# Sixteen-head windowed attention: mask, maxima and normalisation divided anew among the engines

## The reference

```
q, k = rotary(x @ Wq.T), rotary(x @ Wk.T);  v = x @ Wv.T      # 16 heads of 8
scores = q @ k.T / sqrt(8)
mask = (j > i) | (j < i - (WINDOW - 1))                        # WINDOW = 128
p = softmax(where(mask, -inf, scores))
y = (p @ v) @ Wo.T + bo
```

## Time and profile before

| | |
|---|---|
| median of 3 runs | 1532.76 us (1532.57 to 1542.49) |
| the profiled execution, its own time | 1545.9 us |
| its span, first to last instruction | 1544.1 us |
| PE busy | 1269.2 us, 82% |
| DVE busy | 1046.3 us, 68% |
| ACT busy | 808.2 us, 52% |
| POOL busy | 395.7 us, 26% |
| mean granted TensorE clock | 0.911 of 2.4 GHz |

### The profile page before, as it was taken

How to read it: one execution, slowest core, us unless ns; L and a number is a source line. 1 busy time by engine, 2 the same in 40 slices (tenths; PEclk the granted TensorE clock), 3 DMA queues, 4 the chain that set the end, 5 groups by cost and what they waited for, 6 DMA issues and landing times. The chain is left out here.

```text
span 1544.1 us, 23279 instructions
## 1 busy us (share of the span) xinstructions
PE 1269.2 (82%) x8400; PEld 815.4 (53%) x8400; DVE 1046.3 (68%) x2162; ACT 808.2 (52%) x2180; POOL 395.7 (26%) x248
## 2 busy tenths in 40 slices
PE   5767878887998888789775888889689988988986
PEld 4412335884665556456531233579456654655663
DVE  4789976226887787378449998741378879746853
ACT  2466423453764556466627553336276636665663
POOL 0036633412000332032011665360400023202300
PEclk9789978997999989999987888989799999999997
DMA  8300001780000100001010000068400000000000
GB/s 298 123 0 1 0 1 54 254 268 19 2 1 1 35 21 15 1 15 28 2 28 0 1 0 1 1 201 263 130 1 2 1 1 22 22 1 14 22 8 14
DMA packets 42179, 72.21 MB, mean 47 GB/s; under 512 B 3793, under 2 KB 27473, under 8 KB 41810
## 3 DMA queue, kind: packets, MB, share of 16 engines
q1 hardware_dynamic: 28242, 56.30, 10.8%
q10 hardware_dynamic: 11776, 10.23, 2.6%
q0 software_dynamic: 2048, 4.20, 0.9%
HBM read 51.19 MB, written 13.24 MB: 42 GB/s over the span
## 5 line engine op out<-in xcount | busy, mean ns | idle before, releaser
L912 POOL TENSOR_TENSOR scratch<-scratch 128x1024 f32<-128x1024 f32 x64 | 149.7, 2353 | 140.4 <-DVE scratch L883 119.9
L634 POOL TENSOR_TENSOR small<-small,w_const 128x16 f32<-128x16 f32 x32 | 101.1, 3163 | 298.2 <-DVE small L1753 298.2
L731 PE MATMUL psum<-scratch,w_const 128*128 128x512 f32 x256 | 148.8, 713 | 18.5 <-POOL scratch L912 18.4
L883 DVE TENSOR_TENSOR_SCAN scratch<-psum,scratch 128x512 f32<-128x512 f32 x128 | 150.1, 1206 | 9.5 <-ACT psum L804 8.9
L634 POOL TENSOR_TENSOR rstd<-rstd,w_const 128x4 f32<-128x4 f32 x32 | 32.8, 1029 | 432.9 <-DVE rstd L596 430.3
L1706 ACT ACTIVATE scratch<-psum,mx 128x128 f32<-128x128 f32 x256 | 90.0, 376 | 72.7 <-DVE mx L1794 71.5
L804 ACT ACTIVATE psum<-scratch,a_neg 128x512 f32<-128x512 f32 x128 | 87.8, 690 | 61.2 <-DVE scratch L883 52.1
L1374 ACT ACTIVATE scratch<-psum,mx 128x256 f32<-128x256 f32 (+1 forms) x256 | 111.2, 465 | 10.0 <-DVE mx L1410 8.4
L720 PE MATMUL psum<-scratch,cb 96*128 96x512 bf16 x128 | 49.7, 428 | 60.6 <-DVE scratch L875 51.3
L1160 ACT ACTIVATE scratch<-psum,scratch 128x128 f32<-128x128 f32 x240 | 68.3, 368 | 54.7 <-PE psum L1101 54.6
L1541 PE MATMUL psum<-w_local,hT 128*128 128x512 f32 x192 | 91.2, 615 | 6.3 <-ACT hT L1523 5.1
(11 more groups left out here) (266 smaller groups left out, 3199.6 us busy)
## 6 DMA issues: line engine op xcount, KB each, us to landing
expert_weights<-in_expert_weights SPq DMA_DIRECT2D x61, 512.0 KB, 5.1
scratch<-scratch ACTq DMA_DIRECT2D x48, 128.0 KB, 2.3
folded_products<-expert_weights SPq DMA_DIRECT2D x8, 512.0 KB, 3.1
folded<-folded_products SPq DMA_DIRECT2D x8, 512.0 KB, 4.7
w_local<-in_local SPq DMA_DIRECT2D x1, 3122.0 KB
sorted_y<-scratch ACTq DMA_DIRECT2D x12, 256.0 KB, 5.6
scratch<-sorted_x SPq DMA_DIRECT2D x4, 704.0 KB, 6.7
scratch<-in_cross SPq DMA_DIRECT2D x1, 2624.5 KB, 12.9
```

Source lines behind the costliest of these rows:

```text
L634: t.eng.tensor_tensor(v, v, W("const", "neg_half").to_broadcast([P, v.shape[1]]), ALU.pow).then_inc(t.s[done], 1)
L731: ins = pe.matmul(sum_banks[c], ident, t.m.hC[:, 2 * ((n - 1) % 2) + c, :], start=(n == 1), stop=(n == NS))
L883: dve.tensor_tensor_scan(t.m.hs[:, n % 2, c, :], t.ps["dA"], t.m.dBu[n % 2][:, c, :], 0.0, ALU.mult, ALU.add)\
L912: t.eng.tensor_tensor(t.m.hC[:, 2 * (n % 2):2 * (n % 2) + 2, :], t.m.hs[:, n % 2], C, ALU.mult)\
```

## The change

The mask is no longer written by TensorE. The host constant `band3` is negated once into `hidden` (0 or +1e30), q is negated as it is copied out of PSUM, so the banks hold minus the scores, and the instruction that finds the extremum of a block also adds `hidden` to it, writes the sum back to PSUM and keeps the minimum, which is minus the maximum of the masked scores. That is one `tensor_tensor_reduce` for a block of a half, so four for a wide unit and eight for a narrow one, where there was one reduction. The exponential is taken with scale -1. Maxima, exponentials, inverses and probabilities are signalled by half (u) instead of by unit. The normalisation moves to GpSimd: one multiplication of 128x512 for each half, by the inverse sums spread over the columns. `TURNS` is made anew for all engines.

```diff
 TURNS = {
     "dve": [
...
+        1, 1, 5, 1, 3, 1, 1, 1, 1, 1, 1, 1, 1, 1, 1, 1, 3, 1, 2, 2, 1, 1, 3, 1, 2, 2, 1, 1, 7, 5, 8, 8, 7, 7, 7,
+        7, 7, 7, 7, 7, 7, 7, 7, 7, 7, 7, 7, 7, 7, 7, 7, 7, 13, 3, 8, 6, 3, 1, 5, 1, 1, 1, 1, 6, 3, 1, 1, 2, 1, 2,
...
+        hidden = cbv["band3"]
...
-            dve.tensor_scalar(rank_w[:, :], cbv["band3"][:, P:2 * P], -1.0, 1.0 / P, ALU.is_lt, ALU.mult)
+            yield from t.w.step(dve.tensor_scalar(hidden, hidden, -1.0, None, ALU.mult))
+            dve.tensor_scalar(rank_w[:, :], hidden[:, P:2 * P], 1.0, 1.0 / P, ALU.is_gt, ALU.mult)
...
             def turn(n, u):
                 yield
-                if u == 0:
-                    t.w(t.s["prob_ready"])
+                t.w(t.s["prob_ready"])
...
-                    mask = cbv["band3"][:, (2 - nk) * P:2 * P].rearrange("p (o z) -> p o z", o=1)
-                    for bank in banks:
-                        pe.matmul(bank, cbv["ident"], mask.to_broadcast([P, len(gg), nk * P]), start=True, stop=False,
-                                  skip_group_check=True)
...
-                                            start=False, stop=(a == len(gg) - 1), skip_group_check=True)
+                                            start=True, stop=True, skip_group_check=True)
...
-                    yield
-                    t.w(t.s["max_ready"])
-                    if n >= 2:
-                        act.wait_ge(t.s["v_filled"], v0 + 2 * (n - 1))
                     for u in range(2):
+                        yield
+                        t.w(t.s["max_ready"])
+                        if u == 0 and n >= 2:
+                            act.wait_ge(t.s["v_filled"], v0 + 2 * (n - 1))
...
-                                                 accum_out=t.m.sums2[:, c:c + 1])
+                                                 scale=-1.0, accum_out=t.m.sums2[:, c:c + 1])
...
-                    yield
-                    dve.wait_ge(t.s["s_freed"], s0 + 2 * n)
-                    yield from t.w.step(dve.reciprocal(t.m.rinv2[:, c0:c0 + 2 * k], t.m.sums2[:, c0:c0 + 2 * k]))
                     for u in range(2):
-                        for a in range(k):
-                            z, c = t.m.wide_pr[:, (n - 1) % 2, u, a * nk * P:(a + 1) * nk * P], c0 + k * u + a
-                            ins = dve.tensor_scalar(z, z, t.m.rinv2[:, c:c + 1], None, ALU.mult)
-                    ins.then_inc(t.s["prob_ready"], 1)
+                        yield
+                        dve.wait_ge(t.s["s_freed"], s0 + 2 * n - 1 + u)
+                        z = slice(c0 + k * u, c0 + k * u + k)
+                        dve.reciprocal(t.m.rinv2[:, z], t.m.sums2[:, z]).then_inc(t.s["inverse_ready"], 1)
...
-                    t.s_.take()
-                    dve.tensor_reduce(t.m.mx2[:, c0:c0 + 2 * k], pair, X, ALU.max, negate=True)\
-                        .then_inc(t.s["max_ready"], 1)
+                    for u in range(2):
+                        yield
+                        bank = t.s_.take()
+                        for a in range(k):
+                            z, c = bank[:, a * nk * P:(a + 1) * nk * P], c0 + k * u + a
+                            ins = dve.tensor_tensor_reduce(z, z, hidden[:, (2 - nk) * P:2 * P], 1.0, 3.0e38, ALU.add, ALU.min,
+                                                           accum_out=t.m.mx2[:, c:c + 1])
+                        ins.then_inc(t.s["max_ready"], 1)
...
-            for dst in (t.m.wide_qT, t.m.wide_kT):
+            for dst, sign in ((t.m.wide_qT, -1.0), (t.m.wide_kT, 1.0)):
...
-                                 ACT.Copy).then_inc(t.s["a_freed"], 1)
+                                 ACT.Copy, scale=sign).then_inc(t.s["a_freed"], 1)
...
+        def window_band_pool(t):
+            for n in range(len(WPAIRS)):
+                j, nk, i, gg = window_unit(n)
+                k = len(gg)
+                for u in range(2):
+                    yield
+                    t.w(t.s["inverse_ready"])
+                    c, z = 8 * (n % 2) + k * u, t.m.wide_pr[:, n % 2, u, :].rearrange("p (a z) -> p a z", a=k)
+                    by = t.m.rinv2[:, c:c + k].rearrange("p (a o) -> p a o", o=1).to_broadcast([P, k, nk * P])
+                    t.eng.tensor_tensor(z, z, by, ALU.mult).then_inc(t.s["prob_ready"], 1)
+
         def window_pool(t):
+            yield from window_band_pool(t)
             yield from norm_pool(t)
```

More of the change, by code:

```diff
@@ L432, in decoder_kernel @@
                      "sum_filled skip_ready gated_ready gap_ready ratio_ready comb_ready pads_ready "
-                     "rinv_ready max_ready vx_loaded ss_ready root_ready rope_ready sq_ready rst_ready hn_ready "
+                     "rinv_ready inverse_ready max_ready vx_loaded ss_ready root_ready rope_ready sq_ready rst_ready hn_ready "
                      "y_ready stored ")
@@ L1405, in window_band_vector @@
                     k, c0 = len(gg), 8 * (n % 2)
-                    t.skip(s=1)
-                    pair = t.ps["s2"].rearrange("p u z -> p (u z)").rearrange("p (a z) -> p a z", a=2 * k)
-                    yield
-                    t.s_.take()
-                    dve.tensor_reduce(t.m.mx2[:, c0:c0 + 2 * k], pair, X, ALU.max, negate=True)\
-                        .then_inc(t.s["max_ready"], 1)
+                    for u in range(2):
[6 more added lines that the diff above has]
+                        ins.then_inc(t.s["max_ready"], 1)
                 yield
```

## The result

The changed kernel took 1563.76 us (median of 4, 1557.11 to 1570.09) against 1537.62 for the kernel before on the same chip: a ratio of 1.0129, 95% interval 1.0089 to 1.0168. This ratio and all that follow are estimated over the executions of both kernels, without those in a slower state that some executions of either show, and are not the quotient of the medians, which is 1.0170 here. The changed kernel is slower by over 1% where I had forecast 1511 us and a gain. The profiled execution took 1565.0 us.

What follows compares the result with a forecast made beforehand. TensorE was taken to bound the band. 48 wide units at 3.66 - 3.20 us give 22 us, all other terms 0, so the median of 1532.8 becomes 1511 us, range 1495 to 1543.

Steps and rivals of the forecast that it cites:

- The bound: In both passes of the band TensorE is the bound, busy 39.8 and 39.5 of 40 us; VectorE second, GpSimd free.
- The mask leaves TensorE: Wide unit in the band: TensorE loses 0.52 us, 3.66 to 3.14; with loops rubbing, 3.20 taken.
- Rival A: TensorE's whole gain arrives, narrow units too: 56 x 0.52 = 29 us, 1504 us; chance 0.15.
- The combined instruction: VectorE's mask addition with minimum, one block: 0.44 us, between 0.35 and 0.62.
- Rival B: VectorE becomes the band's bound; from 0.74 us a combined instruction the kernel is slower, 1548 us and more; chance 0.20.
- Normalisation on GpSimd: Multiplications in the band take 1.049 us each, two a unit, covered by the other lane's unit of 3.2 us.
- The shared way into SBUF: VectorE's rotary sums and norms at the band's edges slowed beside GpSimd: 0 to 8 us, taken as 0.
- The sum: Over the band's wide units, 48 x (3.66 - 3.20) = 22 us gained.
- the table outside the band: Order of stages outside the band shifts by some yields on every engine; cost taken as 0, kept as a rival.
- The prediction's own last sign: The central number is wrong if stages outside the band change by more than some 5 us.
- Rival C: New table costs outside the band through TensorE's lower granted clock: up to 14 us, 1525 us; chance 0.23.
- Range and chances: Whole kernel: 1495 to 1543 us; faster 0.57, within 1% 0.25, slower 0.18.

Runs made afterwards that it cites:

- the mask products kept: Changed instructions in the old order, TensorE still doing the mask products, which are then overwritten: 0.9976 of the kernel before.
- old order: Changed instructions with the turn table of the kernel before on all five engines, split steps where whole ones stood: 0.9895 and 0.9922 of the kernel before.
- the mask alone: Kernel before plus VectorE adding the mask, normalisation staying on VectorE, old order: 0.9971 of the kernel before; 1.0134 with SyncE's row from the new table.
- the root moved: Changed kernel with GpSimd's inverse root (L640) ahead of the other lane's eight gathers at row 1's window stage: 1.0125 and 1.0104 of the kernel before.
- the new table in row 1 alone: Changed instructions, order of the kernel before through all of row 0, new table in row 1: 1.0016 of the kernel before.

## Why the prediction was wrong, point by point

- **The bound.** Right: TensorE in the band, and the run with the mask products kept shows it from the other side.
- **The mask leaves TensorE, 0.52 us a unit; the unit 3.66 to 3.20.** Right: 3.23 in the changed kernel's trace. Rival A, the whole 0.52, is out with it.
- **The combined instruction, 0.44 us in bounds 0.35 to 0.62.** A little dear: 0.38. It is two instructions, as the Trainium skill says (VectorE: DVE Perf Modes, "Two Vector instructions with no wait between them"), but the accumulator's read of 0.14 us starts with the next main one, so it adds nothing to the upper half of my bounds. Rival B (slower by VectorE, from 0.74) is out: VectorE is busy 31.6 of 40 us in the band.
- **Normalisation on GpSimd.** 1.040 us forecast at 1.049, and covered: in the changed kernel TensorE waits for it nowhere between 430 and 480 us, and once, for 2.0 us, in row 1's band. In the old order it waited 4.6 us for it in row 1's window stage. Both were taken as 0. The Trainium skill's advice against the move (GPSIMD Engine Reference, "4. When to use GPSIMD") would count where GpSimd is at the bound; here, with the mask alone, it is VectorE that is full, and moving the work to the slower engine (1.04 us for what VectorE did in 2 x 0.28) is what lets the other part pay in full.
- **The shared way into SBUF, 0 of 0 to 8 us.** Near enough: the 32 rotary sums (L1506) hold VectorE 10.3 us instead of 7.8, within the bounds; whether that reached TensorE is not shown.
- **The sum, 22 us.** Right in the band of the changed kernel. From the band's first product to its last TensorE takes 115.2 and 105.5 us (row 0, row 1) where the kernel before takes 119.9 and 122.4: 21.6 us less. But its bands begin 28.5 and 37.7 us after the experts' end, against 24.0 and 25.1, so that the two window stages together are only 3.2 us shorter. In the old order the bands take 110.1 and 115.3 us, 16.9 less, and begin in time, so that 15.5 and 16.7 us arrive in the window stages of its two runs. Inside the band the new table pays; at its entry it takes back 17 of those 21.6 us.
- **The step that failed: the table outside the band, "I take 0 and keep it as a rival".** It costs 30 us, 0.0195 of the span. The prediction's own last sign, stages outside the band that change by more than some 5 us, came true in four of them. By stages on TensorE, one execution each: kernel before, changed, and the changed instructions in the old order (first and second run), each stage from the end of the one before:

| stage | before | changed | old order | old order again |
|---|---|---|---|---|
| row 0 to the end of the experts | 347.2 | 357.4 | 350.0 | 350.1 |
| window | 147.0 | 147.0 | 138.8 | 139.2 |
| cross | 31.7 | 29.1 | 32.5 | 29.9 |
| local | 259.9 | 267.5 | 268.6 | 261.5 |
| row 1 to the end of the experts | 303.7 | 302.3 | 308.1 | 306.7 |
| window | 150.6 | 147.4 | 142.1 | 142.9 |
| cross | 29.8 | 37.1 | 29.0 | 32.5 |
| local | 254.6 | 264.9 | 254.5 | 258.2 |

  The last three columns are the same instructions. The changed kernel is 29.1 and 31.7 us above the old order, in five stages against both runs. Part is a wait (the 15 us at row 1's window stage, against 4 in the old order, of which the stage gives some back); part is the clock (60 and 63 us more at 1.2 GHz, with 17.1 and 20.8 us more of busy TensorE in the two local stages). Rival C named this mechanism, with a chance of 0.23, and priced it by two stretches at 14 us at most. That price was too low: that "the trace can't price that" was a reason for a wide price and not for 0.
- **Range and chances.** The upper end of 1543 leaves 32 us over the forecast. The table's 30 us nearly fill that, and the change without its table brings 12 to 16 us by its two ratios, not 22; together they pass the end. The shortfall has two parts that the record shows: 17 us in the band instead of 22, and some 3 to 4 us more than the kernel before in each row's stages ahead of the window, one execution against another.

What stays open: why the clock is at its lower level for longer in the new order. In the local stages TensorE stands no longer than before and yet has the lower clock. It is not those stages' own order alone: with the root moved, twice, row 1's local stage took 256.4 and 256.6 us, and with the new table in row 1 alone 254.3. The runs tie the whole loss to the order and do not say by which pauses the clock's part of it comes.

## What to carry to other kernels

When a change comes with an order made anew, run the changed instructions in the old order too; only that tells which of the two pays, and here the order cost 2 of 100. Price the new order as a cost over the whole span and not over the stage that is edited, and read TensorE's busy time at an equal count of instructions: if it grows, look at the granted clock before you look for a wait. Compare stages over two executions of each kernel; one local stage here moved by 7 us between two executions of the same kernel. If two engines are near the bound, relieve both in one change: in the two window stages one part gave 6.7 us, the other nothing and the two together 16.7.

## What the runs showed of the hardware

- VectorE's combined instruction on 256 columns, PSUM and SBUF in, PSUM and a minimum out: 0.38 us from start to start, its accumulator read (0.14 us) beside the next one.
- 512 KB loads of expert weights landed in a median of 4.9 to 5.4 us on three chips and of 15.3 to 15.4 us on two others; the kernel before took 1562.54 and 1566.1 us on those two, against 1537.6 to 1548.7. It was not traced there, so that the loads are the reason is not shown. Only ratios on one chip compare.
- The order of DMA issues alone: a few steps of lane B one to four places earlier on SyncE, ahead of lane A's expert weights, cost 15.2 and 11.1 us in the two expert stages (109.1 and 110.8 against 93.9 and 99.7, same chip, all else equal), with TensorE's wait for them in row 0 doubled, 12.9 us against 6.7. The mask alone shows it a second time: 1.0134 and 0.9971 are the same kernel but for SyncE's row, with expert stages of 111.6 and 111.0 us against 96.0 and 95.5. What costs is the mismatch with the other engines' order: the changed kernel has the same row of SyncE, and 96.8 us in row 0's.
